# First cross attention of a Perceiver-like kernel on one Trainium2 core: operands turned on the host, and the step schedule regrouped by pairs of key tiles

## What is computed

```python
qh = (layernorm(x) @ Wq.T + bq)    # 16 heads of 8, 64 query rows per batch
kh = (ctx @ Wk.T + bk)             # ctx: 32 x 1601 x 128
vh = (ctx @ Wv.T + bv)
attn = softmax(where(mask != 0, qh kh^T * 8**-0.5, -inf))
x = x + (attn @ vh) @ Wo.T + bo
```

## Time and profile before

| | us |
|---|---|
| median of three runs | 3080.7 (3076.77 to 3083.48) |
| the profiled execution | 3079.37, its span 3077.6 |

### The profile page before, as it was taken

One profiled execution on the slowest core, in us unless ns is written; L12 is line 12 of the kernel. 1 busy time (PEld: TensorE's weight loads), 2 busy tenths in 40 slices (PEclk: granted clock), 3 DMA queues, 4 the chain that ended last, 5 costly groups with the idle time before them and its releaser, 6 DMA issues. The chain is left out here.

```text
span 3077.6 us, 66754 instructions
## 1 busy us (share of the span) xinstructions
PE 2819.4 (92%) x22718; PEld 1618.6 (53%) x22765; DVE 1978.6 (64%) x4504; ACT 1479.6 (48%) x2385; POOL 1906.0 (62%) x1278
## 2 busy tenths in 40 slices
PE   5799999999999978998899999999999997888789
PEld 2355555555555566775344444444444443777356
DVE  5477777777777744114667767767767744776653
ACT  3466666666666522333544444444444434223633
POOL 5487878787878721001488888888888872553500
PEclk8899999999999989998999999999999998999789
DMA  7655555555555210001000000000000000000300
GB/s 184 187 174 193 177 190 181 184 186 179 194 175 188 100 58 1 1 0 39 22 33 21 21 32 21 21 32 21 21 32 21 21 1 9 3 3 2 85 5 10
DMA packets 146463, 233.18 MB, mean 76 GB/s; under 512 B 16787, under 2 KB 85851, under 8 KB 146076
## 3 DMA queue, kind: packets, MB, share of 16 engines
q1 hardware_dynamic: 145180, 228.87, 22.7%
q10 hardware_dynamic: 1152, 2.49, 0.6%
HBM read 147.80 MB, written 83.52 MB: 75 GB/s over the span
## 5 line engine op out<-in xcount | busy, mean ns | idle before, releaser
L444 POOL TENSOR_TENSOR sb_a_acc<-sb_a_acc,sb_a_PT 128x1024 f32<-128x1024 f32 x252 | 596.7, 2368 | 36.6 <-ACT sb_a_PT L522 30.3
L522 ACT ACTIVATE sb_a_PT<-ps_a_SC 128x1024 f32<-128x1024 f32 (+1 forms) x416 | 425.8, 1023 | 315.3 <-PE ps_a_SC L794 291.7
L607 DVE TENSOR_REDUCE sb_a_mx<-ps_a_A 128x1 f32<-128x512 f32 x768 | 506.4, 685 | 97.0 <-PE ps_a_A L771 91.8
L1686 POOL TENSOR_TENSOR sb_a_acc<-sb_a_acc,sb_a_PT 128x512 f32<-128x512 f32 (+2 forms) x384 | 487.5, 1269 | 37.3 <-ACT sb_a_PT L1782 10.9
L1782 ACT ACTIVATE sb_a_PT<-ps_a_SC 128x1024 f32<-128x1024 f32 (+2 forms) x256 | 234.3, 915 | 563.0 <-PE ps_a_SC L2061 329.3
L1875 DVE TENSOR_REDUCE sb_a_mx<-ps_a_A 128x1 f32<-128x512 f32 x384 | 256.5, 679 | 280.1 <-PE ps_a_A L2036 240.1
L2080 PE MATMUL ps_a_PV<-sb_a_PT,sb_a_XN 128*128 128x512 f32 (+2 forms) x896 | 434.3, 601 | 2.2 <-ACT sb_a_PT L1782 0.7
L2061 PE MATMUL ps_a_SC<-sb_a_QX,sb_a_XT 128*128 128x512 f32 (+1 forms) x832 | 396.7, 596 | 0.1
L771 PE MATMUL ps_a_A<-sb_a_KS,sb_a_QS 97*128 97x512 bf16 x768 | 301.9, 394 | 30.6 <-issue 17.7
L794 PE MATMUL ps_a_SC<-sb_a_QS,sb_a_KS 105*128 105x128 bf16 (+1 forms) x3328 | 257.3, 220 | 13.4 <-DVE sb_a_QS L621 13.4
L805 PE MATMUL ps_a_PV<-sb_a_PT,sb_a_V 128*32 128x256 f32 (+1 forms) x3328 | 266.7, 392 | 0.4 <-issue 0.3
(11 more groups left out here) (516 smaller groups left out, 5265.3 us busy)
## 6 DMA issues: line engine op xcount, KB each, us to landing
sb_a_C<-in_ctx_dram SPq DMA_DIRECT2D x64, 768.0 KB
a_KD<-sb_a_K SPq DMA_DIRECT2D x192, 256.0 KB, 4.1
sb_a_KS<-a_KD SPq DMA_DIRECT2D x256, 192.0 KB
a_KD<-sb_a_K SPq DMA_DIRECT2D x192, 144.2 KB, 2.7
sb_a_KS<-a_KD SPq DMA_DIRECT2D x256, 108.2 KB
sb_a_QP<-a_QD ACTq DMA_DIRECT2D x6, 384.0 KB, 14.7
sb_a_up<-in_moe_up_dram SPq DMA_DIRECT2D x1, 2048.0 KB, 7.9
sb_a_dn<-in_moe_dn_dram SPq DMA_DIRECT2D x1, 2048.0 KB, 12.0
```

What stands on the lines that cost most here:

```text
L444: pool.tensor_tensor(acc[:, :], first[:, :], PT[slot(a, j)][:, :], ALU.add).then_inc(s["acc"], 1)
L522: act.activation(PT[slot(a, j)][0:n, :], SC[(a + j) % 2][0:n, :], ACT.Exp).then_inc(s["exp"], 1)
L607: v.tensor_reduce(mx[:, p, c:c + 1], A[u % 2][:, :], AXX, ALU.max).then_inc(s["am"], 1)
L1686: pool.tensor_tensor(acc[a][0:m, :], first, PT[u % 4][0:m, HQ * i:HQ * i + HQ], ALU.add).then_inc(s["acc"], 1)
```

## The change

1. The host turns the context of each batch, with the keys in the same order of tiles as before (`ctx_T`), and the four weight matrices (`L0_xattn_WT`). One transfer loads a batch's `CT` directly. The transposes on PE (L715, L732), their copies on ACT (L478, L486) and the tiles `C`, `CR`, `w0` are gone, and `load` waits for the values that read the buffer last.
2. Steps go by pairs of key tiles (`NG` = 7 groups g). PE's order in group g: scores 2g+2, a unit, scores 2g+3, a unit, keys chunk g (g below 4) or values, `top` (g = 5), one more unit (g above 0), products 2g and 2g+1, the rest of the units, values. Units per group are 4, 5, 5, 5, 7, 0, 0.
3. POOL adds tiles 0, 1, 2, 4, 5, 7, 8, 9 (seven additions). Tiles 3, 6, 10, 11, 12 are multiplied with ones on PE.
4. `top` uses bank `A[0]` in place of `M`. DVE does the units of a group first and the residue after them, and `final` and `invert` at the end of the step. POOL's `divide` moves to the end too.
5. SP's order in a step is spill and stack of the first group, spill and stack of the second, then the load. Before the steps, keys of batch 0 come ahead of the normalisation's transposes, and the load of batch 2 comes later.

```diff
-    COUNT = (0, 2, 2, 2, 2, 3, 3, 3, 3, 3, 3, 0, 0)
+    NG = (NK + 1) // 2
+    COUNT = (4, 5, 5, 5, 7, 0, 0)
+    SUMS = (1, 2, 4, 5, 7, 8, 9)
...
             def load(b, a):
-                wait(sp, s["ct"], 4 * (b - 1))
-                sp.dma_start(C[a][:, :, :], d["ctx_1024"][dsl(b), 0:KF * P, :].rearrange("o (p j) d -> p (o j) d", p=P))\
-                  .then_inc(s[f"ld{a}"], 16)
...
+                wait(sp, s["vp"], 4 * (b - 1))
+                sp.dma_start(CT[a][:, :], d["ctx_T"][dsl(b), :, :].rearrange("o d s -> d (o s)")).then_inc(s[f"ld{a}"], 16)
...
             def step(b, a, n2, n4):
-                if n4:
-                    load(b + 4, a)
                 if n2:
                     for g in range(2):
                         spill(b + 2, a, g)
-                    for g in range(2):
                         stack(b + 2, a, g)
+                if n4:
+                    load(b + 4, a)
...
                     add(b, a, j, i)
-                    if 2 <= j < 6 and n2:
-                        third(b + 2, j - 2)
+                    if n2 and j in (4, 5, 8, 9):
+                        third(b + 2, (4, 5, 8, 9).index(j))
...
+                if not (isinstance(b, int) and b == 0):
+                    divide(b - 1)
...
+            def step(b, a, n1, n2):
+                for g in range(NG):
+                    if g + 1 < NG:
+                        for j in pair(g + 1):
+                            probs(b, a, j)
                     elif n1:
+                        for j in pair(0):
+                            probs(b + 1, 1 - a, j)
+                    if n2 and 1 <= g < 5:
+                        second(b + 2, a, g - 1)
+                    if n2 and g < 4:
+                        keys(b + 2, a, g)
+                    if n2 and g >= 4:
+                        for c in ((0,), (1, 2), (3,))[g - 4]:
+                            values(b + 2, a, c)
...
                 if old:
                     emptied(b - 1)
-                    final(b - 1)
...
+                for g in range(NG):
                     if n1:
+                        for u in units(g):
                             tops(b + 1, u)
+                    if n2 and g < 4:
+                        residue(b + 2, g)
                 if n1:
                     top(b + 1)
                     topped(b + 1, 1 - a)
                 if n2:
                     expand(b + 2, a)
+                if old:
+                    final(b - 1)
+                    invert(b - 1)
...
+            def step(b, a, n1, n2):
+                for g in range(NG):
+                    us = list(units(g)) if n1 else []
+
+                    def maxima(n):
+                        for u in us[0:n]:
+                            tops(b + 1, 1 - a, u)
+                        del us[0:n]
+
+                    if g + 1 < NG:
+                        for j in pair(g + 1):
+                            scores(b, a, j)
+                            maxima(1)
                     elif n1:
+                        for j in pair(0):
+                            scores(b + 1, 1 - a, j)
+                    if n2 and g < 4:
+                        keys(b + 2, a, g)
+                    if n2 and g in (4, 5):
+                        values(b + 2, a, g - 4)
+                    if n1 and g == 5:
                         top(b + 1)
+                    if g > 0:
+                        maxima(1)
+                    for j in pair(g):
+                        products(b, a, j)
+                    if g == NG - 1:
+                        total(b)
+                    maxima(len(us))
+                    if n2 and g in (5, 6):
+                        values(b + 2, a, g - 3)
```

More of the change, by code:

```diff
@@ L253, in stage_xattn0 @@
     sb = lambda n, s, dt=F32: k.sb("a0_" + n, s, dt, ctx)
-    C = [sb(f"C{i}", [P, KF, D]) for i in range(2)]
-    CR = [sb(f"CR{i}", [SR, D]) for i in range(2)]
     CT = [sb(f"CT{i}", [P, S]) for i in range(2)]
@@ L303, in dsl, with units, pair @@
         return bass.ds(b, 1)
-    def units(j):
-        return range(sum(COUNT[:j]), sum(COUNT[:j + 1]))
+    def units(g):
+        return range(sum(COUNT[:g]), sum(COUNT[:g + 1]))
+    def pair(g):
+        return tuple(j for j in (2 * g, 2 * g + 1) if j < NK)
     def summed(b):
-        return (1, 3, 5, 7, 9) if isinstance(b, int) and b == B - 1 else tuple(range(1, PTILE))
+        return (1, 3, 5, 7, 9) if isinstance(b, int) and b == B - 1 else SUMS
     def slot(a, j):
@@ L394, in _ @@
             pieces(1)
+            load(2, 0)
             for g in range(2):
@@ L553, in _ @@
             for c in range(4):
-                turned(1, 1, c)
-            for c in range(4):
                 keys(1, 1, c)
@@ L648, in step @@
                     emptied(b - 1)
-                    final(b - 1)
-                for j in range(1, NK):
-                    if n2 and j < 5:
-                        residue(b + 2, j - 1)
-                    if old and j == 1:
-                        invert(b - 1)
+                for g in range(NG):
                     if n1:
-                        for u in units(j):
+                        for u in units(g):
                             tops(b + 1, u)
+                    if n2 and g < 4:
+                        residue(b + 2, g)
                 if n1:
@@ L749, in values @@
                     wait(pe, s["kt"], 4 * b + 4)
-                elif c < 3 and depth(b) == 1 and not (isinstance(b, int) and b == B - 1):
-                    wait(pe, s["ct"], 4 * b + 6 + c)
                 elif c >= depth(b):
                     wait(pe, s["v"], 4 * b + c - depth(b) + 1)
-                if c == 3:
-                    wait(pe, s["mx"], b)
                 lo, hi = VT[c]
@@ L819, in total @@
                 mm.then_inc(s["sum"], 1)
-            def step(b, a, n1, n2, n3):
-                for j in range(NK):
-                    us = units(j) if n1 else ()
-                    for u in us[0:1]:
-                        tops(b + 1, 1 - a, u)
-                    if j + 1 < NK:
-                        scores(b, a, j + 1)
-                    elif n1:
-                        scores(b + 1, 1 - a, 0)
-                    for u in us[1:2]:
-                        tops(b + 1, 1 - a, u)
-                    if n2 and j < 4:
-                        keys(b + 2, a, j)
-                    if n2 and j in (4, 8, 10):
-                        values(b + 2, a, (4, 8, 10).index(j))
-                    if n3 and j in (5, 6, 7, 9):
-                        turn(b + 3, 1 - a, (5, 6, 7, 9).index(j))
-                    if n1 and j == 11:
-                        top(b + 1)
-                    for u in us[2:]:
-                        tops(b + 1, 1 - a, u)
-                    products(b, a, j)
-                total(b)
-                if n2:
-                    values(b + 2, a, 3)
@@ L860, in _ @@
             for c in range(4):
-                turn(1, 1, c)
-            for c in range(4):
                 keys(1, 1, c)
@@ L865, in _ @@
                 values(1, 1, c)
-            for c in range(4):
-                turn(2, 0, c)
             pe.wait_ge(s["qc"], NT // 4)
```

136 lines of the change are left out of this document (44 added, 92 removed).

## The result

The changed kernel takes 3154.9 us (median of 4, 3152.1 to 3161.5) beside 3080.6 us (median of 4): ratio 1.0245, 95% interval 1.0226 to 1.0265. The profiled execution took 3152.1 us, its span is 3150.3 us. It is slower, as forecast, but by 74 us where I had 27, and outside my range.

The account below looks back on a forecast made before the run. The prediction took PE to be bound by its own list of work, with little waiting. Steps at 32.3 us added 30 us: 3079.4 + 30 + 0 - 2 = 3107, so 3108 us, range 3045 to 3138.

Parts of the forecast that it names:

- All of it is hidden, with 4 us to spare at the tightest place.: SP's spills, stacks and load: first stack landed near 28 us, ahead of the next step's first unit at 32.7.
- the walk: One step followed in PE's order with its waits: ends at 32.4 us, taken as 32.3, +1.07 us per step.
- the term of 2.61 us: From the start of a group's late units through DVE's two reductions and residue to PE's next key chunk: 2.61 us.
- about the same: Rival: PE's waits come out at 3.3 to 3.6 us and cancel the saved work, 3075 to 3087 us; chance 0.08.
- PE's list: PE's own work per step if nothing waited: falls from 29.7 to 27.8 us.
- Seven sums: POOL drops two additions; two more tiles times ones on PE cost 2 x 0.45 = +0.9 us per step.
- Turn: PE's transposes of the context go: three groups of 0.44 and one of 0.28, -1.6 us per step.
- the strips: PE enters and leaves 32-column strips for products in 7 blocks, not 13: -6 x 0.21 = -1.3 us per step.
- Start and step 0: Work before the steps +1 (between -3 and +5), context wait and slow clock in step 0 -3: sum -2 us.
- Last three steps: Steps that lack the load, then keys and values, then both: sum 75 us against 74.64 before, counted as zero.
- The clock: Rival: PE's clock falls at the four late units of g4 in each step, adding 56 us: 3164 us; chance 0.05.
- The stack comes late: Rival: stacked keys arrive late by a few us per step, or the walk misses a wait: 3125 to 3150; chance 0.07.

Follow-up runs that it names:

- Without the trip: Changed kernel without the spills and stacks of key pieces in the steps and without the waits for them: 3077.6 us, ratio 0.9992.
- the kernel without loads: Changed kernel without the loads of the context from batch 4 on, spills and stacks kept: 3080.9 us, ratio 1.0003.

## Why the prediction was wrong where it was

**The step that failed: "All of it is hidden, with 4 us to spare at the tightest place."** The part on SP followed one trip, from the third piece to the first unit, in the right order. Held against the trip from 338.37, its terms come out so (the walk counts from the first scores, 0.45 us ahead of the first unit, which is taken off here): third piece ready at 13.05, measured 14.4; landing of the spill 4.1, measured 5.2 from its last issue; eight issues 5.6, measured 5.83; landing of the stack 4, measured 8.06 (364.13 to 372.19). Landed at 27.55, measured 33.8. The largest error is the last, 4.1 of the 6.3 us by which the trip is longer than I had it. It used up nearly all of what I had to spare, and PE is ready for its next first unit sooner than I had reckoned, since its own work is 31.3 and not 32.3 us. The late third piece is the low clock of that step (below): in the next one, at a clock of 1.00, it is ready 12.85 us behind the first unit (372.19 to 385.04), and the trip still takes 33.0. I gave the stack the landing time of a spill, though no row showed one: the kernel before never waited for a stack in its steps, so its trace has no landing there, and I should have left that term open upwards.

Second, I gave the spill its landing of before, though the change itself puts an 800 KB load directly ahead of it. Without the load it lands after 2.7 us, with it after 5.7 (medians of the 256 KB transfers). The Trainium skill ("DMA: Bandwidth & Descriptors", Queues, rings and completion order) says that the increment of a semaphore lands only after every earlier write of the same DMA engine. A small transfer behind a large one would then report late, and the medians here agree with that; they can't tell it from engines that simply share their time among the transfers.

Third, and behind both: I looked at the trip of one group, and not at SP's round as a list of its own, as I had done for PE. In the changed kernel it is 4.7 + 0.7 + 5.8 + 2.9 + 0.7 + 5.9 + 0.4 = 21 us of issues and 11.2 us for two landings (325.3 us in 29 steps), with 1.8 us of waits for the makers ((43.6 + 4.7 and 3.7 more) / 29): 34, and the period is 33.9. The issues of that list could have been added up from the timeline of before. Its landings could not: with the medians of before (4.1 and 2.7) the round comes to 21 + 6.8 = 28 us, still hidden under the step. What made it the bound is that SP now waits for two landings in each round, and that both spills stand behind something large, the first behind the load and the second behind the first stack. That the load delays the first is shown by the runs without it there; for the second the stack as the cause is read from its place and was not tested. The last transfer of a second spill lands after 1.8 us in the kernel before (issued at 438.0) and after 7.8 in the changed one (issued at 366.8).

**The engines' walk: +1.07 us per step, measured +0.06.** This is the second term that failed; put right by itself it would have brought the forecast down to some 3080, the time of before. Without the trip a step is 31.30 against 31.24. PE's groups were priced right (V, S, T, P, O stand at their distances, and the tail is 7.20 as in the walk). DVE's chain was not: two units in a row take 1.29 us, not 1.38, and the second begins 0.60 after the first. DVE in a step of the kernel without loads:

```profile
391.09 1.29 DVE L586 TENSOR_REDUCE sb_a_mx<-ps_a_A 128x1 f32<-128x512 f32 x2 [1.49 <-PE ps_a_A L730]
392.30 0.74 DVE L569 SCALAR_TENSOR_TENSOR sb_a_RK<-ps_a_M,sb_bk,sb_a_K 128x512 f32<-128x512 f32 x1
392.96 1.28 DVE L586 TENSOR_REDUCE sb_a_mx<-ps_a_A 128x1 f32<-128x512 f32 x2
```

Reduction to reduction to residue is 0.60 + 0.61, and the residue is done 0.66 after it began as far as the next one is concerned. So the term of 2.61 us to each key chunk is 2.43: in PE's timeline of that step the late units start at 390.66 and K at 393.09. K ahead of products, priced at 1.06 in g0, is 0.95. In the same kernel's step that starts at 356.07, PE runs ahead of the walk by 0.31 us at the second key chunk, by 0.50 and 0.70 at the third and fourth, by 0.88 at the first values and by 1.07 at the end of the burst in g4. That is the difference between the walk (32.38) and the step (31.30). I had read 0.69 from a row of four reductions that took 2.76, so started 0.69 apart there; a term that stands eight times in a sum needs more than one row. The trace of before has many rows of two that take 1.28 us, so start 0.59 apart, and the changed kernel's has rows of three:

```profile
426.62 1.28 DVE L607 TENSOR_REDUCE sb_a_mx<-ps_a_A 128x1 f32<-128x512 f32 x2
```

```profile
151.25 1.87 DVE L588 TENSOR_REDUCE sb_a_mx<-ps_a_A 128x1 f32<-128x512 f32 x3
```

The rival "about the same" described the engines correctly: its waits of 3.3 to 3.6 us are what the step without a trip has, 31.30 less PE's list of 27.8.

**The parts of the sum.** Seven sums: +0.9 predicted, +0.87 measured alone. Turn: -1.6 predicted on PE's list, -0.44 per step measured alone, since waits took its place. The order of pairs was not run alone; if these two simply add up, it is worth 31.30 - 31.24 - 0.87 + 0.44 = -0.4 us, against the -1.3 for the strips and +3.0 of waits in my sum. Start and step 0: -2 predicted (its bounds were added up wrongly: -3 to +5 and -3 give -6 to +2); the first read of PV moved from 138.61 to 135.19, so -3.4, with PE's wait for the first stack at 19.3. Last three steps: 75 predicted, 74.64 before, 76.0 after (33.32 + 26.29 + 16.42; without the trip 73.9).

**The clock.** That rival was given 5 in 100 and a wrong cause. The bursts of units did not lower the clock: without the trip it is 1.00 from 107 to 1060 us. It fell only at waits for the transfer, and not at each. Ahead of and behind the wait of 2.48 us that ended at 338.37, and behind one of 3.02 us that ended at 508.27:

```profile
330.00:334.00 4.00, 4.00 (x72) 2.70 (x68) 3.50 (x7) 1.80 (x4) 0.21 (x1) 1.00 0.76 278
...
338.30:342.60 4.30, 4.23 (x28) 1.62 (x28) 1.36 (x2) 1.71 (x2) 1.45 (x1) 0.65 0.21 57
...
508.30:512.30 4.00, 3.88 (x39) 2.06 (x39) 2.11 (x4) 1.71 (x2) 1.23 (x1) 1.00 0.18 53
```

The granted clock behind the first is 0.65, a mixture of 1.2 and 2.4 GHz, and from start to start the keys and products take 1.49 and 1.87 us there where they take 0.96 and 1.00 a step later. It fell at 8 of the 25 waits in the steps, the shortest of them 1.85 us long, and stayed at 1.00 behind the other 17, ten of which were as long or longer; no run here says why. Of the 77 us between the changed kernel and the one without the trip, 55 are waits for keys in the steps. The other 22 can be estimated from the clock: eight windows of 8 us behind these eight waits have a granted clock of 0.79 (five) and 0.57 (three), so 8 x (5 x 0.21 + 3 x 0.43) = 18.7 us of work at full speed are missing in them. That is most of the 22, if PE had work throughout. The Trainium skill ("TensorE: Matmul & The Clock Gate", HAM oscillation) describes a loop in which a wait for a transfer in each round lets the clock fall each time. This trace agrees in part: in 8 of 25 waits.

**The rivals and the range.** "The stack comes late" by a few us per step was the right mechanism, priced at 3125 to 3150 with 7 in 100. The measured 3154.9 is 5 us above that price: the waits of 55 us were within it, and the slower clock came on top. The range ended at 3138 because I gave this rival less than 0.10. It would have taken the stack's landing and the two longer spill landings, which no row of before showed, to make it the forecast. The marks I had set down named it: a wait of PE on a transfer inside the steps. That the direction came out as forecast was luck: the reason I gave, 32.3 us of the engines' own work, is not why the kernel is slower.

**Left open.** Whether the two landings could be taken off SP by issuing the stacks from another engine's queue was not tried.

## What to carry to other kernels

Add up the round of each queue that issues transfers as you add up an engine's list: issues, and the landings that it waits for in line. If a change sets a dependent transfer right behind its source, each round pays that landing in full. Don't take the landing from a kernel with another order: here it grew with what stood ahead of it in the queue. A gain for an engine shows nothing while another loop sets the period, so take the suspected loop away once and measure what is left.

## What the runs showed of the hardware that I had not expected

- Six transfers of 16 partitions by eight rows take SP 2.7 us to issue, eight of 96 partitions 5.8. But the kernel with them keeps the DMA engines busy at 0.87 while moving 144 GB/s; the changed kernel, with the 96-partition form, shows a share of 0.51 at 168 GB/s, both from 300 to 500 us. The cheaper form for the queue is the dearer one for the DMA engines.
- The last of the 144 KB transfers of a second spill, issued right behind a stack, lands after 7.8 us; in the kernel before, with no stack ahead of it, after 1.8.
- Waits of PE of up to 3.0 us for a transfer left the granted clock at 1.00 (behind the one that ended at 508.27), while one of 1.85 us (ended at 270.55) was followed by 0.60.
- Reductions that follow one another on DVE without a wait start 0.60 us apart, though one alone is shown with 0.69.
